# A chunked GRU with routed splines on one core: input loads cut in four, first loads asked for earlier, two more weight stages, and the difference formed ahead of the transpose

## The reference

```python
def cell(h, x):                       # scanned over 1024 positions, batch 4, width 1024
    gi = x @ W_ih + b_ih
    gh = h @ W_hh + b_hh
    i_r, i_z, i_n = jnp.split(gi, 3, axis=-1)
    h_r, h_z, h_n = jnp.split(gh, 3, axis=-1)
    r = jax.nn.sigmoid(i_r + h_r)
    z = jax.nn.sigmoid(i_z + h_z)
    n = jnp.tanh(i_n + r * h_n)
    h_new = (1.0 - z) * n + z * h
    return (h_new, h_new)
...
# each state is layer-normed, routed by signs to one of 64 tiles, and a 16-wide slice
# of it goes through that tile's spline: out = state + delta
x = x + ffn(scan(cell, cond_2048, x))
```

## Time and profile before

| | us |
|---|---|
| median of 3 runs (lowest, highest) | 2580.62 (2580.52, 2583.52) |
| the profiled execution | 2581.43 |
| its span, first to last instruction | 2579.6 |

### The profile page before, as it was taken

How to read it: one execution, slowest core, us unless ns; L and a number is a source line. 1 busy time by engine, 2 the same in 40 slices (tenths; PEclk the granted TensorE clock), 3 DMA queues, 4 the chain that set the end, 5 groups by cost and what they waited for, 6 DMA issues and landing times. The chain is left out here.

```text
span 2579.6 us, 82162 instructions
## 1 busy us (share of the span) xinstructions
PE 2352.5 (91%) x35300; PEld 1284.4 (50%) x35300; DVE 1290.6 (50%) x2644; ACT 663.1 (26%) x1334; POOL 188.5 (7%) x376
## 2 busy tenths in 40 slices
PE   7999999999999869999999959999999999967734
PEld 3444444444444335555665536666666666633311
DVE  4322121211113347676655544666666666877765
ACT  2200000000001223333333322333333333355520
POOL 0000000000000000000000000111111111121217
PEclk9999999999999979999999979999999999999955
DMA  6593131313133434443333332444444444477712
GB/s 208 180 348 131 54 122 54 122 53 123 52 141 123 155 102 150 140 150 116 126 118 126 118 131 71 118 122 117 117 115 115 116 116 119 131 221 222 226 44 4
DMA packets 169331, 330.27 MB, mean 128 GB/s; under 512 B 17296, under 2 KB 79168, under 8 KB 168192
## 3 DMA queue, kind: packets, MB, share of 16 engines
q1 hardware_dynamic: 134800, 267.48, 32.0%
q10 hardware_dynamic: 24192, 44.05, 4.6%
q0 software_dynamic: 10240, 17.31, 4.4%
HBM read 222.13 MB, written 156.77 MB: 147 GB/s over the span
## 5 line engine op out<-in xcount | busy, mean ns | idle before, releaser
L526 PE MATMUL rz_bank<-w_hi,hi 128*32 128x512 f16 x6912 | 420.7, 386 | 113.6 <-DVE hi L817 54.8
L270 DVE SCALAR_TENSOR_TENSOR out_stage<-acc,bias_row 128x512 f32<-128x512 f32 x168 | 115.6, 691 | 609.6 <-PE acc L326 609.6
L526 PEld LDWEIGHTS rz_bank<-w_hi,hi 128*32 128x32 f16 x6912 | 175.3, 98 | 299.6 <-DVE hi L817 64.6
L324 PE MATMUL acc<-w_hi,x_even 128*128 128x512 f16 x768 | 293.6, 382 | 17.8 <-DVE x_even L262 11.2
L325 PE MATMUL acc<-w_hi,x_even 128*128 128x512 f16 x768 | 293.6, 382 | 0.0
L326 PE MATMUL acc<-w_lo,x_even 128*128 128x512 f16 x768 | 293.3, 382 | 0.0
L526 PE MATMUL rz_bank<-w_lo,hi 128*32 128x512 f16 x4096 | 243.4, 379 | 0.0
L526 PE MATMUL rz_bank<-w_hi,lo 128*32 128x512 f16 x4096 | 243.2, 379 | 0.0
L782 DVE SCALAR_TENSOR_TENSOR sums<-rz_bank,gi 128x512 f32<-128x512 f32 x176 | 121.3, 689 | 227.1 <-PE rz_bank L526 219.4
L649 ACT ACTIVATE rz<-sums 128x512 f32<-128x512 f32 x176 | 110.6, 628 | 461.6 <-DVE sums L782 461.1
L526 PE MATMUL n_bank<-w_hi,hi 128*32 128x256 f16 x6912 | 228.4, 274 | 0.0
(11 more groups left out here) (187 smaller groups left out, 2652.6 us busy)
## 6 DMA issues: line engine op xcount, KB each, us to landing
gi<-gi_scratch SPq DMA_DIRECT2D x176, 384.0 KB
gi_scratch<-out_stage ACTq DMA_DIRECT2D x168, 256.0 KB, 2.1
gi<-sums_scratch SPq DMA_DIRECT2D x40, 512.0 KB
xstage<-in_xT SPq DMA_DIRECT2D x32, 512.0 KB, 6.6
y<-in_x_rows SPq DMA_DIRECT2D x32, 512.0 KB, 7.7
hs_scratch<-h SPq DMA_DIRECT2D x128, 128.0 KB
x_keep<-hs_scratch SPq DMA_DIRECT2D x32, 512.0 KB, 6.7
y<-hs_scratch POOLq DMA_DIRECT2D x32, 512.0 KB, 6.9
```

The lines of the kernel that those rows point to most:

```text
L270: nc.vector.scalar_tensor_tensor(out=out_stage[:, tb], in0=acc[e % BANKS][:], scalar=UNSCALE, in1=bias_row[:].rearrange("p q f -> p (q f)" ...
L324: nc.tensor.matmul(acc[e % BANKS][:], hi, wh, start=k == 0, stop=False)
L526: last = nc.tensor.matmul(bank[q * COLS:(q + 1) * COLS, 0:b - a], state[:, s, j], w[:, j, q * QW + a:q * QW + b], start=first and j == 0, ...
```

## The change

Four things. `load_inputs` asks for a set-step's inputs in four transfers, one for each quarter of 32 partitions and 96 KB, each adding 16 to the semaphore. The first input loads of either set (slot 0) and the first four late loads are asked for by SP in the input phase, behind the last weight load; for that the inputs' buffer, `late_ring` and their semaphores are made before the phase, and `xstage` and `sign_b` share their room with them. The recurrent weights get two more stages in the half of `xstage` that the inputs don't take. In the difference set-steps VectorE forms old_less = 256 z_old - kept state, then 256 new_n + old_less in 16 bits, transposes that into `hi`, and only then makes h; h is not transposed there. For that the kept state is saved untransposed, and `act_keep` waits for h. The diff, cut to its core:

```diff
--- before.py
+++ after.py
@@ -78,6 +78,19 @@
 LATE_STEPS = KB // SETS
 
 
+def load_inputs(sp, t, gi_dram, pos, s, u):
+
+    for q in range(QUARTERS):
+        sp.dma_start(t["gi"][q * COLS:(q + 1) * COLS, s, u, 0:QW],
+                     gi_dram[bass.ds(pos * POS + s * COLS, COLS), q * QW:(q + 1) * QW]).then_inc(t["gi_loaded"][s][u], 16)
+
+
+def load_late(sp, t, late_w, cb, k):
+
+    sp.dma_start(t["late_ring"][:, k % RING], late_w[k, :, bass.ds(cb, 1)].rearrange("p o a f -> p (o a) f"))\
+      .then_inc(t["late_loaded"][k % RING], 16)
+
+
 def input_product(nc, ctx, t, W_ih, W_hh, b_ih, b_hh, xT, gi_dram, slopes, gamma, beta, gamma_t, beta_t,
                   out_scale, sign_dram, x_rows, hs_dram, late_w):
@@ -89,7 +102,7 @@
 
     w_hi, w_lo = t["w_hi"], t["w_lo"]
     wstage = sb("wstage", [P, 2, KX, CW])
-    xstage = sb("xstage", [P, KB, BW])
+    xstage = t["stage"][:].rearrange("p (k n) -> p k n", k=KB)
     x_even = sb("x_even", [P, 2, KB, BW], F16)
     x_hi, x_lo = ([x_even[:, part], t["x_keep"][:, part]] for part in range(2))
     out_stage = sb("out_stage", [P, TB, CW])
@@ -100,9 +113,19 @@
     slope_sign = sb("slope_sign", [NT, SLICE])
     acc = [ctx.enter_context(nc.psum_tensor(f"acc{i}", [P, CW], F32)) for i in range(BANKS)]
 
-    sign_b = sb("sign_b", [P, D])
-
-    w_loaded = [sem(f"w_loaded{i}") for i in range(2)]
+    sign_b = t["late_ring"][:].rearrange("p r a f -> p (r a f)").bitcast(F32)[:, 0:D]
+
+
+    STAGES = 4
+    stages = [wstage[:, 0], wstage[:, 1], xstage[:, 4:4 + KX], xstage[:, 6:6 + KX]]
+    w_loaded = [sem(f"w_loaded{i}") for i in range(STAGES)]
+
+    def stage_of(j):
+
+        if j < PIECES:
+            return j % 2, j // 2 + 1
+        turn, at = divmod(j - PIECES, STAGES)
+        return at, turn + 1 + (PIECES // 2 if at < 2 else 0)
     x_loaded = [sem(f"x_loaded{i}") for i in range(XPARTS)]
     x_hi_ready, x_lo_ready = sem("x_hi_ready"), sem("x_lo_ready")
     w_hi_ready, w_lo_ready = sem("w_hi_ready"), sem("w_lo_ready")
@@ -124,10 +147,15 @@
         @block.sync
         def _(sp):
             def load_w(j, src, m):
-                if j >= 2:
-                    sp.wait_ge(w_hi_ready, j - 1)
-                    sp.wait_ge(w_lo_ready, j - 1)
-                sp.dma_start(wstage[:, j % 2], w_piece(src.rearrange("(k p) n -> p k n", p=P), m)).then_inc(w_loaded[j % 2], 16)
+                at, times = stage_of(j)
+                if at >= 2 and times == 1:
+                    sp.wait_ge(x_hi_ready, NBLK * XPARTS)
+                    sp.wait_ge(x_lo_ready, NBLK * XPARTS)
+                elif times > 1:
+                    behind = j - (2 if j < PIECES + 2 else STAGES)
+                    sp.wait_ge(w_hi_ready, behind + 1)
+                    sp.wait_ge(w_lo_ready, behind + 1)
+                sp.dma_start(stages[at], w_piece(src.rearrange("(k p) n -> p k n", p=P), m)).then_inc(w_loaded[at], 16)
 
             def load_x(n, k):
 
@@ -196,12 +224,22 @@
 
             for m in range(PIECES):
                 load_w(PIECES + m, W_hh, m)
+
+            for b in range(TB):
+                sp.wait_ge(gi_stored[b], 2 * CBLOCKS * 16)
+            for s in range(SETS):
+                load_inputs(sp, t, gi_dram, LEN - WARM, s, 0)
+            sp.wait_ge(late_w_stored, 16 * 2 * KB)
+            sp.wait_ge(rows_ready, 1)
+            for k in range(RING):
+                load_late(sp, t, late_w, 0, k)
             sp.wait_ge(rows_loaded, 10 * 16)
             sp.wait_ge(rows_begun, (NBLK - 1) * 16)
 
         def split_w_hi(act, j, m):
-            act.wait_ge(w_loaded[j % 2], 16 * (j // 2 + 1))
-            nc.scalar.activation(w_piece(w_hi, m), wstage[:, j % 2], ACT.Copy, scale=W_SCALE).then_inc(w_hi_ready, 1)
+            at, times = stage_of(j)
+            act.wait_ge(w_loaded[at], 16 * times)
+            nc.scalar.activation(w_piece(w_hi, m), stages[at], ACT.Copy, scale=W_SCALE).then_inc(w_hi_ready, 1)
 
         def split_x_hi(act, n, buf, k):
             act.wait_ge(x_loaded[k // KX], n * 16 + 16)
@@ -254,7 +292,7 @@
 
         def split_w_lo(dve, j, m):
             dve.wait_ge(w_hi_ready, j + 1)
-            nc.vector.scalar_tensor_tensor(out=w_piece(w_lo, m), in0=wstage[:, j % 2], scalar=W_SCALE,
+            nc.vector.scalar_tensor_tensor(out=w_piece(w_lo, m), in0=stages[stage_of(j)[0]], scalar=W_SCALE,
                                            in1=w_piece(w_hi, m), op0=ALU.mult, op1=ALU.subtract).then_inc(w_lo_ready, 1)
 
         def split_x_lo(dve, n, buf, k):
@@ -425,6 +463,9 @@
     z_old = sb("z_old", [P, SETS, QF])
     new_n = n_sum
 
+    old_less = sums[:, :, 0:QF]
+    diff = [sums[:, s, RZ:RZ + QF // 2].bitcast(F16) for s in range(SETS)]
+
     gap_all = rn
     gap = sb("gap", [P, 1])
@@ -664,9 +707,9 @@
             nc.scalar.activation(saved[:, s, 0], sums[:, s], ACT.Copy, scale=SUM_SCALE).then_inc(saved_hi_ready[s], 1)
 
         def act_keep(act, it, u, s):
-            act.wait_ge(turned[s], steps_to(it, u))
+            act.wait_ge(h_ready[s], steps_to(it, u))
             act.wait_ge(state_stored[s], it * 32 + (u * 16 + 32 - WARM_HEADS * 16))
-            nc.scalar.activation(state_out[:, s], flat(h_turned[:, s]), ACT.Copy, scale=S_SCALE).then_inc(state_out_ready[s], 1)
+            nc.scalar.activation(state_out[:, s], h[:, s, u], ACT.Copy, scale=S_SCALE).then_inc(state_out_ready[s], 1)
 
         def act_diff(act, it, u, s):
             act.wait_ge(hi_ready[s], steps_to(it, u) + 2)
@@ -797,26 +840,34 @@
             nc.vector.tensor_tensor(z_old[:, s], rz[:, s, QF:RZ], h_old, ALU.mult).then_inc(z_old_ready[s], 1)
             if after_old:
                 after_old()
+            if mode in (DIFFS, LAST):
+                dve.wait_ge(z_old_ready[s], n)
+                dve.wait_ge(warm_state_loaded[s][u], from_diffs(it) * 8 + 16 * (1 + u))
+                nc.vector.scalar_tensor_tensor(out=old_less[:, s], in0=z_old[:, s], scalar=S_SCALE, in1=warm_state[:, s, u],
+                                               op0=ALU.mult, op1=ALU.subtract).then_inc(old_less_ready[s], 1)
             dve.wait_ge(not_z_ready[s], n)
             dve.wait_ge(n_ready[s], n)
             nc.vector.tensor_tensor(new_n[:, s], not_z[:, s], n_act[:, s], ALU.mult).then_inc(new_n_ready[s], 1)
             dve.wait_ge(z_old_ready[s], n)
             dve.wait_ge(new_n_ready[s], n)
+            if mode in (DIFFS, LAST):
+                dve.wait_ge(old_less_ready[s], from_diffs(it) + (u + 2))
+                nc.vector.scalar_tensor_tensor(out=diff[s], in0=new_n[:, s], scalar=S_SCALE, in1=old_less[:, s],
+                                               op0=ALU.mult, op1=ALU.add).then_inc(diff_made[s], 1)
+                dve.wait_ge(diff_made[s], from_diffs(it) + (u + 2))
+                if mode == DIFFS:
+                    dve.wait_ge(diff_seen[s], from_diffs(it) + (u + 1))
+                nc.vector.transpose(flat(hi[:, s]), diff[s]).then_inc(hi_ready[s], 1)
             if mode not in (HEADS, KEPT):
                 dve.wait_ge(h_stored[s][u], it * 16 + (16 - pair_of(0, 0) * 16))
-            nc.vector.tensor_tensor(h_new, new_n[:, s], z_old[:, s], ALU.add).then_inc(h_ready[s], 1)
-            dve.wait_ge(h_ready[s], n)
             if mode == KEPT:
                 dve.wait_ge(state_out_ready[s], it * 2 + (u + 1 - WARM_HEADS))
+            nc.vector.tensor_tensor(h_new, new_n[:, s], z_old[:, s], ALU.add).then_inc(h_ready[s], 1)
+            if mode in (DIFFS, LAST):
+                return
+            dve.wait_ge(h_ready[s], n)
             nc.vector.transpose(flat(h_turned[:, s]), h_new).then_inc(turned[s], 1)
-            if mode in (DIFFS, LAST):
-                dve.wait_ge(turned[s], n + (seeds - 1))
-                dve.wait_ge(warm_state_loaded[s][u], from_diffs(it) * 8 + 16 * (1 + u))
-                if mode == DIFFS:
-                    dve.wait_ge(diff_seen[s], from_diffs(it) + (u + 1))
-                nc.vector.scalar_tensor_tensor(out=flat(hi[:, s]), in0=flat(h_turned[:, s]), scalar=S_SCALE, in1=warm_state[:, s, u],
-                                               op0=ALU.mult, op1=ALU.subtract).then_inc(hi_ready[s], 1)
-            elif mode != HEADS:
+            if mode != HEADS:
                 dve_low(dve, s, n + seeds)
             if mode == KEPT:
                 dve.wait_ge(saved_hi_ready[s], it * 2 + (u + 1 - WARM_HEADS))
@@ -988,6 +1039,7 @@
                         tile(i, (DIFFS, DIFFS), True)
                     for s in range(SETS):
                         dve.sem_inc(lo_ready[s], WARM_FULL + 1)
+                        dve.sem_inc(turned[s], WARM_FULL + 1)
                         dve.sem_inc(rz_sum_ready[s], WARM_FULL)
                         dve.sem_inc(hn_ready[s], WARM_FULL)
@@ -1110,13 +1162,8 @@
 
             passes(pool, one_pass)
 
-        def load_late(sp, cb, k):
-            sp.dma_start(late_ring[:, k % RING], late_w[k, :, bass.ds(cb, 1)].rearrange("p o a f -> p (o a) f"))\
```

(18 more changed lines are left out.)

9 lines of the change are left out of this document (5 added, 4 removed).

## The result

The changed kernel takes 2521.1 us (median; 2520.5 to 2523.1) where the kernel before, beside it, takes 2580.7: a ratio of 0.9768, 95% interval 0.9751 to 0.9785, or 59.6 us less. The forecast was 2521.5. The profiled execution has a span of 2518.8 us against 2579.6, 60.8 less.

A forecast was written before the change was run, and what follows sets the result against it. PE was taken to bound most of the kernel, with time to gain in five places; -4.5 - 19.2 - 14.2 - 16 - 7 + 1 = -59.9 us, from 2581.4 to 2521.5 us, range 2515 to 2528 (55%).

The forecast's parts named there:

- Part 1: Seam after the input products: with four weight stages the splits run without waiting, so PE starts earlier; -4.5 us.
- Part 2: First late block: PE's 17.24 us wait goes and the late matmuls run at full clock; -19.2 us.
- Part 3: Input loads: four transfers spread over 16 DMA engines instead of four, for +1.3 us of issues a load.
- Part 4: Second half of the 40 kept set-steps: faster landings let PE set the pitch, not SP's loop; -14.2 us.
- Part 5: Seam before the first pass: PE's stop of 31.18 us falls to 14.9 to 17.2; -16 us.
- Part 6: Difference set-steps: a shorter chain gives -7 us over ten tiles; h later after the last step, +1 us.
- rival E: Difference steps: the 16-bit transpose runs at a copy's pace, 2515 us; 4%.
- Rival C: Difference steps gain nothing, through one more VectorE operation or the token load: 2528 to 2532 us; 17%.
- Rival B: Input loads spread, but the landing falls only to 4.5 us or an issue costs more: 2535 us; 13%.
- A: SP's loop in the kept steps: the split spreads nothing or landings stay behind the load, 2608 us; 6%.
- D: Input phase: SP ends it, its loads aren't hidden, PE starts up to 5 us later, 2526 us; 5%.
- The signs of being wrong: SP over 5 us between store and reload, four input issues over 2.5 us, or ScalarE's sum waiting for token load.

The follow-up runs named there:

- two_stages: Changed kernel with two stages for the recurrent weights instead of four: 2530.1 us.
- two_transfers: Changed kernel with each input load as two transfers of two quarters (64 partitions) each: 3075.0 us, one run.
- h_first: Changed kernel with h = new_n + z_old moved ahead of the difference and its transpose in the difference steps: 2528.9 us.
- not_early: Changed kernel with the first input and late-weight loads asked for at the late stage's start, as before, still in four transfers: 2530.6 us.
- only_four: Kernel before with one edit, each input load as four transfers of 32 rows: 2540.0 us.
- gates_first: Changed kernel with the next set-step's gates ahead of the last difference's square on ScalarE in the difference steps: 2513.5 us.

## Why the prediction was right

**Part 1**, -4.5: measured -4.6 (8.46 us of idle time against 13.09). PE's start came at 901.90 for a forecast 902.5; 0.4 of that is no gain of the change, since the last input matmul ended 0.4 earlier (893.44 against 893.87). In the other kernels with four stages PE starts at 901.1 to 903.8 behind the same 8.46. That SP is hidden holds, but only with the four stages (two_stages).

**Part 2**, -19.2: measured -19.3, from PE's start to the second set's products (909.52 - 901.90 against 933.85 - 906.96). The 17.24 us are gone, the 12 late matmuls take 2.69 us instead of 5.21, and the 0.6 given back for a later rise of the clock was needed: the first 64 matmuls take 0.5 us more. The runs say more than the part did: the early request alone ends the wait, the four transfers alone leave 6.26 of 17.24 us.

**Part 3**, the spread: one, two and four transfers show 0.25, 0.13 and 0.80 for the DMA share. The issue cost, 1.3 us more a load, measured 1.74 to 1.89 us against 0.6: +1.1 to +1.3. The Trainium skill gives a rule in DMA: Bandwidth & Descriptors (Why a DMA increments its semaphore by 16 and not by 1): the largest number up to 16 that divides the slowest dimension of both sides. The trace agrees for outermost counts of two and four (two and four packets under way at once), and for 32 rows, where the rule gives sixteen, up to 16 are. The "Don't bother" of the same page (Rules for kernel authors) speaks of halves that each use all sixteen engines. Here the whole transfer used four, so it didn't apply; that parts share their engines is seen in two_transfers.

**Part 4**, -14.2: kept set-steps at 7.80 from first to last, -14.4 (39 pitches of 7.81 from 1192.15 end at 1496.7, not 1496.6, so the forecast's own rows give 14.0). Landings of 1.8 to 2.4 us for a forecast of 2.5 to 3.0.

**Part 5**, -16: the stop is 14.29 us, under the 14.9 to 17.2 forecast, since the shifts land in about 1.3 us behind their last issue (1488.04 + 3.35 to 1492.71), not 1.8 to 4.1.

**Part 6**, -7 and +1: -4.8 and +0.6. This is the mis-sized term. In short steps the forecast of -0.20 to -0.25 held (-0.20 and -0.31). In long ones it was -0.1, and nothing came. The prediction's own three terms (0.36 + 0.25 - 0.66) make -0.05, which it rounded up, and with it the sum of a tile. By the rows of one with the scalings: h 0.34 more, old_less 0.28 more between z_old and new_n, and 0.60, not 0.66, back between new_n and hi (1.76 to 1.16): +0.02. A sum of terms of 0.3 to 0.6 us had an error as large as its result. The 16-bit transpose takes 0.45 us as taken, which ends rival E.

**Rival C** was there as a mechanism, without its price. The sum now waits for the token load, 6.4 us in ten tiles, but in time that ScalarE had to spare: the square behind it isn't later, and the short steps differ by the same 0.1 us in h_first, where nothing waits for that load. Its other half, one more VectorE operation, did take the gain of the long steps. Rival B fell with the landings, A with the shares, D with the idle 8.46.

**The signs of being wrong.** Two of the three came true without harm. The sum waits for the token load, as said. And SP's time between store and reload stays over 5 us (1472.40 to 1477.96), since it now waits for the saved sums, which VectorE finishes at 1477.35, and not for the landing. A sign should have named what SP waits for.

The errors are small and of both signs: +2.2 and -0.4 in part 6, -0.9 in part 5, -0.2 in parts 1 and 2 together, -0.2 in part 4, -0.4 in the input phase, which the change doesn't touch, and -0.8 in the full steps, where I had nothing. The last is the clock, and chance: the first set-step of the first pass takes 9.19 us at a granted clock of 0.85, against 10.52 at 0.74 before; in other kernels with the same stop of 14.29 us in front it takes 9.15 to 9.86. That the sum, -59.9, is so near to the -60.8 of the traces is in part luck.

## What to carry to other kernels

When a small store lands late, look at what is queued ahead of it and at the DMA share while that is in flight: 0.25 or 0.13 says that a transfer sits on few engines, and cutting it so that each piece begins with many rows can be worth more than its extra issues cost, as long as the issuing queue isn't the one that sets the pitch. A wait that goes must be followed to what is next in line: behind the square stood the gates, behind the gates the DMAs. A new wait costs nothing as long as what stands behind it on its engine isn't later for it. And where an edit adds and removes operations of about equal length on an engine that is always at work, expect nothing there; its gain lies only in the steps in which that engine waits.

## What the runs showed of the hardware

- The cost of a wrong cut is steep: cut in two transfers of two quarters, the input loads run at 48 GB/s, and the kernel takes 3075 us (one run) instead of 2521 with four.
- The fewer engines a load sits on, the more it delays others: the 384 KB store of the sums lands in 9.6, 6.9 and 2.4 us beside input loads at a DMA share of 0.13, 0.25 and 0.80.
- The 512 KB token load of the full steps, which the change doesn't touch, gains too: its landing falls from 6.7 to 3.9 us, and is 6.8 with one transfer. PE is full there, so the time doesn't show it.
- The same stage differs from run to run by the clock after a short stop. At the start of the kept stage PE stands 3.8 us in each of the kernels of the table but two_transfers. In some profiled executions it goes on at the full clock, and its first 32 matmuls take 1.91 us. In others they take 2.4 to 3.6 us: 2.79 at a granted clock of 0.66 in not_early, 3.61 at 0.50 in only_four. Among kernels whose kept stage has the same instructions, that stage then takes 328.2 us (not_early, 1175.33 to 1503.48) or 329.3 (gates_first) against 326.5. The changed kernel, then not_early:

```profile
1167.65 1.91 PE L569 MATMUL rz_bank<-w_hi,hi 128*32 128x512 f16 x32 [3.79 <-DVE late_out L811]
```
```profile
1175.33 2.79 PE L565 MATMUL rz_bank<-w_hi,hi 128*32 128x512 f16 x32 [3.79 <-DVE late_out L807]
```
